# VectorE's share of the exponentials: three key tiles instead of two, pieces of 2048 columns, a 16-bit range step and a polynomial of degree 5

## The reference

```python
def wl_step(acc, wl):
    cpm, iw = wl                                  # cos of the channel's phase by head, its weight
    Qw, Kw = Q * m, K * m                         # m = cpm[None, :, None, None]
    scores = jnp.einsum('bhqd,bhkd->bhqk', Qw, Kw) * SCALE
    scores = scores * jnp.cos(KERR * scores * scores)
    attn = jax.nn.softmax(scores, axis=-1)
    out = jnp.einsum('bhqk,bhkd->bhqd', attn, V)
    return (acc + out * iw, None)
```

## Time and profile before

| | |
|---|---|
| median of 3 runs | 3687.97 us (3685.47 to 3691.52) |
| profiled execution, span from first to last instruction | 3702.4 us |
| ScalarE busy | 3523.5 us, 95% |
| VectorE busy | 2935.0 us, 79% |
| TensorE busy (matmuls) | 2654.8 us, 72% |
| mean granted TensorE clock | 0.887 of full speed |

### The profile page before, as it was taken

The page is one execution under the profiler, slowest core; times in us unless marked ns, Lnnn a source line. Parts: engine busy times, 40 slices in busy tenths (PEclk is TensorE's granted clock), DMA queues, the critical chain, the costliest instruction groups (busy, mean ns, idle before and its releaser), DMA issues.

```text
span 3702.4 us, 49245 instructions
## 1 busy us (share of the span) xinstructions
PE 2654.8 (72%) x19639; PEld 813.5 (22%) x19639; DVE 2935.0 (79%) x3858; ACT 3523.5 (95%) x634; POOL 55.9 (2%) x206
## 2 busy tenths in 40 slices
PE   5767777677777776777777777767777777777763
PEld 2222222222221221222222222222222222222222
DVE  6788777788777777777788788788878888888787
ACT  6999999999999999999999999999999999999981
POOL 0000000000000000000000000000000000000000
PEclk7998988999988889888889889898988989889896
DMA  1000000000000000000000000000000000000001
GB/s 46 1 1 1 1 1 1 1 1 1 1 1 1 1 1 1 1 14 1 1 3 1 4 2 4 2 4 1 2 4 2 4 2 1 4 2 4 2 23 32
DMA packets 19220, 16.64 MB, mean 4 GB/s; under 512 B 4177, under 2 KB 16866, under 8 KB 18722
## 3 DMA queue, kind: packets, MB, share of 16 engines
q1 hardware_dynamic: 18130, 12.54, 1.2%
q10 hardware_dynamic: 720, 0.34, 0.0%
q0 software_dynamic: 128, 0.26, 0.0%
HBM read 7.76 MB, written 5.37 MB: 4 GB/s over the span
## 4 chain that ended last, share of the span: by engine, by line
ACT 58%; issue 31%; PE 8%; DVE 3%; DMA 0%; SPq 0%; ACTq 0%; POOL 0%; DVEq 0%; POOLq 0%
ACT probs L595 57%; PE psum L1198 7%; DVE x_p L666 0%; DVE m_pad L768 0%; PE psum L717 0%; DVE probs L841 0%; DVE probs L1104 0%; DMA probs<-in_L_attn_bv_dram 0%; ACT probs L612 0%; PE psum L817 0%; DMA out_dram<-probs 0%; PE psum L829 0%; SPq L402 0%; DVE q_s L652 0%; PE psum L812 0%
## 5 line engine op out<-in xcount | busy, mean ns | idle before, releaser
L595 ACT ACTIVATE probs<-s_t,c_head 128x8192 f32<-128x8192 f32 (+1 forms) x512 | 3488.0, 6898 | 52.1 <-PE psum L1198 50.8
L1198 PE MATMUL psum<-probs,v_pad 128*27 128x512 f32 x15872 | 2196.2, 681 | 669.9 <-ACT probs L595 617.0
L1198 PEld LDWEIGHTS psum<-probs,v_pad 128*27 128x27 f32 x15872 | 557.3, 118 | 2038.7 <-issue 1355.5
L666 DVE SCALAR_TENSOR_TENSOR x_p<-x_p,x_y 128x1024 f32<-128x1024 f32 x640 | 781.9, 1222 | 14.2
L1383 DVE COPY o_sb<-psum 128x512 f32<-128x512 f32 x192 | 132.8, 692 | 253.3 <-PE psum L1198 240.4
L768 DVE TENSOR_REDUCE m_pad<-psum 128x4 f32<-128x2048 f32 x132 | 301.6, 2286 | 3.9
L789 DVE COPY s_t<-psum 128x2048 f32<-128x2048 f32 x130 | 296.9, 2284 | 5.1 <-PE psum L747 4.1
L697 PE MATMUL psum<-x_p,v_pad 128*27 128x512 f32 x512 | 159.6, 707 | 186.2 <-DVE x_p L684 186.2
L759 DVE TENSOR_SCALAR v_t<-psum,b_head 128x512 f32<-128x512 f32 x33 | 24.8, 751 | 207.3 <-PE psum L717 207.3
L684 DVE SCALAR_TENSOR_TENSOR x_p<-x_p,x_2k 128x1024 f32<-128x1024 f32 x128 | 156.8, 1225 | 4.4
L1182 PE MATMUL psum<-ident,o_sb 128*128 128x128 f32 x768 | 122.2, 282 | 47.8 <-DVE weighted L1371 47.8
(11 more groups left out here) (243 smaller groups left out, 988.5 us busy)
## 6 DMA issues: line engine op xcount, KB each, us to landing
x_next_dram<-weighted SPq DMA_DIRECT2D x1, 1024.0 KB, 3.9
x_group<-x_next_dram SPq DMA_DIRECT2D x1, 1024.0 KB, 4.8
loop_memory<-in_L_attn_x_dram SPq DMA_DIRECT2D x8, 128.0 KB, 2.2
x_dram<-loop_memory SPq DMA_DIRECT2D x8, 128.0 KB, 1.8
out_dram<-loop_memory SPq DMA_DIRECT2D x8, 128.0 KB, 1.8
x_dram<-probs SPq DMA_DIRECT2D x2, 512.0 KB, 3.6
out_dram<-probs SPq DMA_DIRECT2D x2, 512.0 KB, 3.6
s_t<-in_L_ffn_ew_dram SPq DMA_DIRECT2D x3, 256.0 KB
```

Of the source, the lines that this page charges most:

```text
L595: nc.scalar.activation(probs[:, w % 2, n0:], s_t[:, p, n0:], ACT.Exp, scale=c2_head[:, p, w:w + 1]).then_inc(s["exp_done"], 1)
L666: link(nc.vector.scalar_tensor_tensor(out=x_p[:], in0=x_p[:], scalar=c, in1=x_y[:], op0=ALU.add, op1=ALU.mult))
L1198: last = nc.tensor.matmul(products_of(wg)[L * b:L * b + SLOTS * A, :], v_pad[:, p, b * T + kt, c0:c0 + SLOTS * A], probs[:, w % 2, at:at + ...
```

## The change

The last channel's first three key tiles, 6144 columns, become VectorE's, and ScalarE keeps 2048 of its 8192. VectorE does them in three pieces of 2048 columns, one key tile each. A piece is eight instructions: scale and clamp with a 16-bit integer as output, which rounds (x_n, in the memory of x_2k); the remainder, from the scores and x_n; an add and a multiply on the 16-bit integers in place, which make them the bits of the power of two; a first step (x_y + c) x_y of a polynomial whose leading coefficient is 1; three steps of Horner's rule; and the last one with the power of two. With the leading coefficient taken out, VectorE's exponentials are K times the true ones, so ScalarE adds ln K to the exponent of the last channel as a bias column; the factor leaves the division by the sums. The parts of a piece are cut anew (PART_LINKS) and stand at other steps. The products have four matmuls, at steps 6, 12 and 15. The scratch for indirect transfers becomes 4096 bytes in size; x_y, x_p and x_2k are twice as wide.

```diff
@@ -38,22 +38,23 @@
 W_GROUPS = [(0, 3), (3, 3), (6, 3), (9, 3), (12, 3), (15, 1)]
-DVE_KT = 2
-X_BATCHES = 2
-X_COLS = X_BATCHES * S
-PIECES = DVE_KT * NB // X_BATCHES
+DVE_KT = 3
+X_COLS = NB * S
+PIECES = DVE_KT
...
 LOG2_E = float(np.log2(np.e))
-BIASED_MAGIC = float(1.5 * 2 ** 23 + 127)
 LOWEST_Y = -126.0
-EXP2 = (1.0000000005541674, 0.6931472057372656, 0.24022646890630472, 0.05550328776967869, 0.009618488957523083,
-        0.00133999312182961, 0.00015345811891707452)
-PART_LINKS = (0, 4, 7, 9)
-
-PIECE_STEPS = {0: (0, 0), 2: (0, 1), 3: (0, 2), 4: (1, 0), 5: (1, 1), 7: (1, 2), 8: (2, 0), 9: (2, 1), 10: (2, 2),
-               11: (3, 0), 12: (3, 1), 13: (3, 2)}
-PRODUCT_STEPS = {4: 0, 8: 1, 11: 2, 15: 3}
+EXP2 = (1.0000000720243355, 0.6931469729420637, 0.24022120187733026, 0.05550713283174646, 0.009675540932398906,
+        0.0013276471959171143)
+LN_K = float(np.float32(-np.log(EXP2[5])))
+K_EXP2 = tuple(c * float(np.exp(LN_K)) for c in EXP2[:5])
+PART_LINKS = (0, 2, 3, 4, 5, 6)
+
+PIECE_STEPS = {0: (0, 0, 2), 2: (0, 2, 3), 3: (0, 3, 4), 4: (0, 4, 5),
+               5: (1, 0, 1), 7: (1, 1, 3), 8: (1, 3, 4), 10: (1, 4, 5),
+               11: (2, 0, 1), 12: (2, 1, 3), 13: (2, 3, 5)}
+PRODUCT_STEPS = {6: 0, 12: 1, 15: 2}
 NWG = len(W_GROUPS)
@@ -114,6 +115,8 @@
         x_2k = sb("x_2k", [P, X_COLS], BF16)
+        x_n = x_2k[:].bitcast(I16)
+        ln_k = sb("ln_k", [P, 1])
         c2_last = sb("c2_last", [P, H])
@@ -591,8 +594,8 @@
-                                n0 = DVE_KT * NB * S if w == W - 1 else 0
-                                nc.scalar.activation(probs[:, w % 2, n0:], s_t[:, p, n0:], ACT.Exp,
+                                n0, bias = (DVE_KT * NB * S, ln_k[:, 0:1]) if w == W - 1 else (0, 0.0)
+                                nc.scalar.activation(probs[:, w % 2, n0:], s_t[:, p, n0:], ACT.Exp, bias=bias,
                                                      scale=c2_head[:, p, w:w + 1]).then_inc(s["exp_done"], 1)
@@ -657,45 +660,41 @@
             n = u * PIECES + piece
-            link = Linked(dve, s["piece_chain"], n * PART_LINKS[3] + PART_LINKS[part])
-
-            a = [c * (-1) ** i for i, c in enumerate(EXP2)]
-
-            def horner(*coefficients):
-                for c in coefficients:
-                    link(nc.vector.scalar_tensor_tensor(out=x_p[:], in0=x_p[:], scalar=c, in1=x_y[:], op0=ALU.add, op1=ALU.mult))
+            link = Linked(dve, s["piece_chain"], n * PART_LINKS[5] + PART_LINKS[part])
+            scores = s_t[:, p, piece * X_COLS:(piece + 1) * X_COLS]
+            scale = c2_last[:, bass.ds(h, 1)]
+
+            def horner(c):
+                link(nc.vector.scalar_tensor_tensor(out=x_p[:], in0=x_p[:], scalar=c, in1=x_y[:], op0=ALU.add, op1=ALU.mult))
             if part == 0:
-                scores = s_t[:, p, piece * X_COLS:(piece + 1) * X_COLS]
-                link(nc.vector.tensor_scalar(x_y[:], scores, c2_last[:, bass.ds(h, 1)], LOWEST_Y, ALU.mult, ALU.max))
+                dve.wait_ge(s["piece_ready"], n + 1)
+                link(nc.vector.tensor_scalar(x_n, scores, scale, LOWEST_Y, ALU.mult, ALU.max))
+                link(nc.vector.scalar_tensor_tensor(out=x_y[:], in0=scores, scalar=scale, in1=x_n, op0=ALU.mult, op1=ALU.subtract))
+            if part == 1:
+                nc.vector.tensor_scalar(x_n, x_n, 127.0, 128.0, ALU.add, ALU.mult)
                 dve.wait_ge(s["piece_used"], n + 1)
-                link(nc.vector.tensor_scalar(x_p[:], x_y[:], BIASED_MAGIC, None, ALU.add))
-                low_halves = x_p[:].bitcast(I16).rearrange("p (n o) -> p n o", o=2)[:, :, 0:1]
-                nc.vector.tensor_scalar(x_2k[:].bitcast(I16).rearrange("p (n o) -> p n o", o=1), low_halves, 7, None,
-                                        ALU.logical_shift_left)
-                link(nc.vector.scalar_tensor_tensor(out=x_y[:], in0=x_p[:], scalar=BIASED_MAGIC, in1=x_y[:],
-                                                    op0=ALU.subtract, op1=ALU.subtract))
-                link(nc.vector.tensor_scalar(x_p[:], x_y[:], a[6], None, ALU.mult))
-            if part == 1:
-                horner(a[5], a[4], a[3])
+                link(nc.vector.scalar_tensor_tensor(out=x_p[:], in0=x_y[:], scalar=K_EXP2[4], in1=x_y[:], op0=ALU.add, op1=ALU.mult))
             if part == 2:
-                horner(a[2], a[1])
-                nc.vector.scalar_tensor_tensor(out=x_p[:], in0=x_p[:], scalar=a[0], in1=x_2k[:],
+                horner(K_EXP2[3])
+            if part == 3:
+                horner(K_EXP2[2])
+            if part == 4:
+                horner(K_EXP2[1])
+                nc.vector.scalar_tensor_tensor(out=x_p[:], in0=x_p[:], scalar=K_EXP2[0], in1=x_2k[:],
                                                op0=ALU.add, op1=ALU.mult).then_inc(s["piece_ready"], 1)
...
-            pe.wait_ge(s["piece_ready"], u * PIECES + (piece + 1))
+            pe.wait_ge(s["piece_ready"], u * PIECES + (piece + 2))
             if piece == 0:
...
                 pe.wait_ge(s["o_copied"], u * NWG + 2)
-            kt, b0 = piece * X_BATCHES // NB, piece * X_BATCHES % NB
-            for i in range(X_BATCHES):
-                b = b0 + i
-                last = nc.tensor.matmul(products_of(NWG - 1)[L * b:L * b + SLOTS * A, :], v_pad[:, p, b * T + kt, VPAD:VPAD + SLOTS * A],
-                                        x_p[:, i * S:(i + 1) * S], start=(kt == 0), stop=False)
+            for b in range(NB):
+                last = nc.tensor.matmul(products_of(NWG - 1)[L * b:L * b + SLOTS * A, :], v_pad[:, p, b * T + piece, VPAD:VPAD + SLOTS * A],
+                                        x_p[:, b * S:(b + 1) * S], start=(piece == 0), stop=False)
             last.then_inc(s["piece_used"], 1)
@@ -1240,6 +1239,7 @@
             nc.vector.memset(half_pi[:], float(np.pi / 2))
+            nc.vector.memset(ln_k[:], LN_K).then_inc(s["piece_ready"], 1)
             nc.vector.memset(comb[:, NT - 3:NT - 1, :], 0.0).then_inc(s["sw3_zeroed"], 1)
@@ -1375,7 +1375,9 @@
                                 if w in PIECE_STEPS:
-                                    piece_dve(dve, *PIECE_STEPS[w], u, p, u - g * H)
+                                    piece, part0, part1 = PIECE_STEPS[w]
+                                    for part in range(part0, part1):
+                                        piece_dve(dve, piece, part, u, p, u - g * H)
                                 if w in LAST_OF:
@@ -1419,7 +1421,7 @@
-    nc = _bacc.Bacc("TRN2", target_bir_lowering=False, num_devices=1)
+    nc = _bacc.Bacc("TRN2", target_bir_lowering=False, num_devices=1, dynamic_dma_scratch_size=4096)
     arrays, args = {}, {}
```

## The result

The changed kernel takes 3711.19 us, median of 4 runs (3708.83 to 3713.61), beside 3687.52 (3685.47 to 3691.52, 4 runs) for the kernel before: ratio 1.0055, interval 1.0038 to 1.0072, slower by more than 0.2%. The forecast's likeliest case, 3691, did not come; the rival in which the delay behind the loop's edge adds up did in kind, but not in its size, 3701 (3709 with a dear price that did not come true). The time is at the upper end of the range, 3711.

A forecast was written before the change was run, and what follows sets the result against it. ScalarE is busiest, but exponential 14 and then its PV set unit boundaries. ScalarE 0, TensorE 0, first-half pieces 0, pairs +1, end +1.6: about +3 us on the median 3687.97, giving 3691; range 3664 to 3711.

The forecast's parts named there:

- likeliest case: Whole kernel: about 3 us slower, 3691 us (3685 to 3696), within 0.2% of the kernel before; chance 0.46.
- the rival in which the delay behind the loop's edge adds up: Nothing given back: 1.6 us at each of 7 loop edges and the end, 12.8 in all, 3701; chance 0.27.
- dear price: VectorE's first piece instruction, with 16-bit output, at 2.28 us instead of 1.28; with adding delay 21 us, 3709.
- ScalarE's saving is worth 0: Last channel's exponential 1.71 us shorter, 54.8 over 32 units, all hidden by the PV of channel 14 at unit boundaries.
- about 50 us: Sign to look for: ScalarE's idle time before its exponentials rises by this much, released by PV.
- TensorE 0: Products go from 8 to 12 matmuls a unit, last channel's PV from 8 to 4: same 256, no waits of any length.
- VectorE's prices: Piece instructions of 2048 columns: scalar_tensor_tensor 2.28 us, first with 16-bit output 1.28, 16-bit add and multiply 1.23.
- Where VectorE is late: Step walk: in time in first half; second half's first units level with PV 14, second units' step-14 copy 3.4 us late.
- How much of 1.6 arrives?: Delay at PV 0 behind the loop's edge: half given back in each of three PVs, boundaries shift once by about 1 us.
- Pairs longer than 221.9: Sign against the prediction: a pair of units in the second half takes more than the 221.9 us seen before.
- The point named in advance: Behind the loop's edge, delay adds up once PV 0 ends over 7.0 us behind the end of exponential 0.
- The end: Behind the last pair nothing takes VectorE's delay back: 1.6 us longer.

The follow-up runs named there:

- e1: Changed kernel with ScalarE's exponential of the last channel at 4096 columns again, 2048 of them unused: 3709.57 us, ratio 1.0053.
- e6: e3 with ScalarE's exponential of the last channel at 4096 columns again, 2048 of them unused: 3656.87 us, ratio 0.9908.
- e3: Changed kernel with the pieces' parts at every step from 0 to 13 and the products at steps 5, 10 and 15: 3658.36 us, ratio 0.9915.
- e10: e3 without its third piece: two tiles on VectorE, products at steps 5 and 10, 4096 columns on ScalarE: 3658.01 us, ratio 0.9916.
- e5: e3 with the third piece from channel 14 instead of 15, its last two parts at step 12, product at step 14: 3617.43 us, ratio 0.9804.
- e9: e5 with the three pieces tile 0 of channels 15, 11 and 14, each leaving ScalarE 6144 columns: 3610.59 us, ratio 0.9788.
- e2: Changed kernel with two VectorE feed-forward stages at steps 6 and 7 of the second half's second units, not 7 and 11: 3681.9 us, ratio 0.9981.
- r1: Kernel before, unchanged, profiled a second time: 3693.53 us, span 3691.3 where the first profiled execution spanned 3702.4.
- e7: Changed kernel with only the products of pieces 0 and 1 moved, from steps 6 and 12 to 5 and 11: 3701.08 us, ratio 1.0024.
- e8: Changed kernel without its third piece, products at steps 6 and 15, ScalarE's last exponential 4096 columns: 3673.09 us, ratio 0.9959.

## Why the prediction was right in its range and wrong in its likeliest case

**ScalarE's saving is worth 0: right**, shown three times (e1 beside after, e6 beside e3, e10 beside e3), and by e5 and e9 from the other side: with ScalarE's columns in all the same, 2048 of the saved ones taken from channel 14 bring 41 us, and 2048 each from channels 14 and 11 bring 48. The idle time that rose by "about 50 us" is no confirmation: it came to 50.6 by luck, as the sum given above. The fast gap was forecast 1.87 and is 1.77, because the exponential with a bias column takes 2.08 us, not 1.98; "the bias column adds nothing that the rows could show" was wrong by 0.10.

**TensorE 0: right**, with one addition: in the second units of the second half the last product waits 0.7 to 2.6 for VectorE, 11.8 in all.

**VectorE's prices: right but for one.** 2.29, 2.35 and 1.28 were measured for 2.28, 2.28 and 1.28. The 16-bit add and multiply was forecast 1.23 and took 0.69. The Trainium skill's figure ("VectorE: DVE Perf Modes", the perf-mode tier table), 693 ns, agrees with this trace. The busy time rose by 62 us where 99 were forecast.

**Where VectorE is late: right for the second units, a little short for the first.** In the first half the copy at step 14 is on time, in the second unit of pairs in the second half it isn't. The walk put it at 2266.0, 114.4 us into the unit that began at 2151.60; the trace has it 114.8 into its unit. Errors cancel there: step 12 was 0.54 too dear, and two waits of VectorE, 0.53 for the scores of step 10 and 0.29 in the feed-forward stage, were not in the walk.

```profile
2224.99 2.29 DVE L788 COPY s_t<-psum 128x2048 f32<-128x2048 f32 x1 [0.53 <-PE psum L746]
...
2254.92 0.16 DVE L859 SCALAR_TENSOR_TENSOR loop_memory<-loop_memory 128x2 f32<-128x2 f32 x1 [0.29 <-DVE loop_memory L861]
```

In the first units, forecast level with PV 14, the copy is 0.8 to 2.9 late in seven of eight; no exponential waits for that.

**"How much of 1.6 arrives?": this step failed.** The prediction let each PV give half of the delay back, so that it would shift the boundaries once and "does not add up". It recurs. At the seven edges PV 0 begins 3.6 to 5.8 us later in its unit than in the first execution of before, 31.9 in all, and exponential 2 begins 29.3 later: 2.6 of 31.9 are given back, not half. From the start of unit 17 to the start of unit 31, seven pairs, took 1553.1 us before and 1563.3 after: 1.5 a pair. That this is close to the 1.6 that the rival charged is luck, since it is 4.2 more at exponential 2 less 2.7 of slow boundaries. Against the second execution of before, 1546.3, it is 2.4 a pair. Pairs longer than 221.9 were the prediction's own sign of being wrong. The pairs' constant 221.9, which was the argument against the rival, was read wrongly. In the first execution of before the second unit was held at 111 us by a PV 14 that ran partly at 1.2 GHz (its timeline and the window around it, granted clock 0.72):

```profile
2257.19 5.75 PE L1198 MATMUL psum<-probs,v_pad 128*27 128x512 f32 x34 [2.74 <-ACT probs L595]
```

```profile
2256.00:2262.00 6.00, 4.81 (x32) 1.34 (x36) 4.95 (x24) 4.73 (x2) 0.00 (x0) 0.72 0.00 0
```

In the second execution the first four of these pairs take 221.8 too, but with the gaps at exponential 6 and in front of the next unit, and the last two take 218.4:

```profile
2191.74 66.84 ACT L595 ACTIVATE probs<-s_t,c_head 128x8192 f32<-128x8192 f32 x10 [1.77 <-PE psum L1198]
2260.31 108.95 ACT L595 ACTIVATE probs<-s_t,c_head 128x8192 f32<-128x8192 f32 x16 [1.73 <-PE psum L1198]
```

So a constant sum said nothing of what a later PV 0 would do; why both executions come to 221.8 is not shown. In after that PV 14 runs at full clock, the second unit takes 109.3 to 109.6, and the next one begins 1.7 sooner. That takes nothing off the pair, since VectorE's and TensorE's work at the edge doesn't come sooner with it: the copy is now 5.5 into the unit rather than 3.4, the transposes run at 1.2 GHz, and PV 0 starts at 12.7. The point named in advance, PV 0 ending over 7.0 behind the end of exponential 0, is passed by 3.5 to 5.9 us at every edge. A gap moved from the boundary to exponential 2 and grew on the way; e2, which takes the lateness out, finds pairs of 218.4 below both. The 1.6 itself was too small: PV 0 was forecast 10 into its unit and begins at 12.5 to 14.5.

**The end: a term too small.** Forecast +1.6; behind exponential 15 it is 8.2 longer than in the first execution of before, 8.6 than in the second. In the last unit the copy at step 14 comes 11.1 behind the end of exponential 14, before 5.45. Of the 8.2, 1.6 are only the shorter exponential 15, after which the count begins. e2 takes back 6.9 of it by the same edit, so it is the same lateness. The smaller scratch for indirect transfers, put at 0, has no part in it: e3 has the same scratch and an end of 109.8.

**The sum** went by the first profiled execution's gaps. By r1 another execution has 9.9 us less of them, which hid that before's second half could be at 1764.5. The range held partly by luck: its upper end, 3711, stood on a dear price of the 16-bit output (2.28, measured 1.28), while the loss came from a delay two and a half times as large as forecast, less slow boundaries that went away.

**Open.** Why the first half has six slow boundaries in after and e7, one in e3 and none in e6 and e10; and how much of before's slow boundaries in the second half went away with the change and how much differs from one execution to the next. The products' steps alone don't do it (e7), nor the third piece (e8, 1759.3); what e3 changes beside them is the parts' places on VectorE, but no run shows through which wait they would act.

## What to carry to other kernels

Ask of a saved microsecond which instruction ends last at the boundary where the engine waits: 2048 columns were worth nothing in the channel whose exponential runs beside the pacing PV; moved to the channel before it they were worth 41 us. A period that stays constant while the gaps in it vary isn't proof that a delay is absorbed; find out what holds the period, since when that goes, the delay is next. When work on a second engine is enlarged, the step to look at is the last one before a loop's edge or a wait with many things behind it, and the cheap test is to move other work out of it.

## What the runs showed of the hardware

- A bias column costs 0.10 us in each exponential: 3.79 with and 3.69 without at 4096 columns. The Trainium skill ("ScalarE: Activation LUTs", What ACT_TABLE_LOAD costs) gives about 93 ns for each operand of this kind; the trace agrees.
- An add and multiply on neighbouring 16-bit integers, in place, takes 0.687 us for 2048 columns; the shift that read every other one took 0.694 for 1024. A tensor_scalar with 16-bit output and 32-bit input takes 1.277 for 2048 columns, the 1.28 that was drawn from L670. A scalar_tensor_tensor gained nothing from a 16-bit operand (L673, 2.352 us, and L685, 2.292, beside 2.287 for L668).
- Two profiled executions of the same kernel differed by 11.1 us of span, 9.9 of it in gaps in front of exponentials, and the gaps stood at other steps (exponential 6 in place of the boundaries).
